# Layer-norm scalars and router steps moved from GpSimd to ScalarE and VectorE in a Mamba and mixture-of-experts kernel

## The chip, the cores and the metric

One core of one Trainium2 chip. The time is the device time of one execution, in microseconds, median of several runs. Of the kernel before three runs were timed: 4454.32 us median, 4450.94 to 4455.48.

## What is computed

```python
x = x + 0.5 * ffn(layernorm(x))        # x: 16 sequences of 512 tokens, 128 wide
x = x + mamba(layernorm(x))            # 4 layers, state 16, inner width 256, then @ Wout + bout
x = x + 0.5 * ffn(layernorm(x))

def layernorm(x):                      # no weights
    return (x - mean(x)) / sqrt(var(x) + 1e-5)
def ffn(x):                            # 8 experts, 2 of them per token, hidden 344
    logits = x @ Ws + bs
    w, idx = top_k(logits, 2);  w = softmax(w)
    combine = sum(one_hot(idx, 8) * w[..., None], axis=1)
    ...                                # silu(x Wg) * (x Wu), then Wd, weighted by combine
def mamba_layer(x):
    ...                                # rmsnorm, Win, causal conv, silu, Wx, softplus
    h = exp(delta * A) * h + (delta * u) * B;  y = h . C      # along the 512 tokens
    ...                                # y * silu(z) @ Wblk, added to x
```

## The kernel before

All inputs are laid out on the host, all weights stay in SBUF. One program runs three kinds of work through the same five in-order queues.

**The scans.** Each of the 16 sequences has 4 Mamba layers: 64 phases of 128 "ticks", one after the other. A phase has 8 units of 4 tiles (128 x 512 each). For a unit, POOL (GpSimd) multiplies delta*u by B (L962, 128 x 2048, signal `dbu_ready`), ACT (ScalarE) makes exp(delta*A) of each tile into one of three PSUM banks (L609), DVE (VectorE) scans each tile (L778), POOL (L953) or, for 12 of the 32 tiles, DVE (L783) multiplies by C, and PE (TensorE) sums into y (L449).

**The feed-forward units.** 32 of them (two per sequence), each 8 experts of 32 ticks: PE broadcasts the expert's gate (L458, "gb"), DVE scales the input by it (L851, "xs"), PE makes g and u tiles (L466, L475, L480) in two PSUM banks a and b in turn, ACT takes silu (L637, between two table loads), DVE multiplies (L858), PE multiplies by Wd (L487).

**The norms and the router.** 48 layer norms: DVE bn_stats and bn_aggr (L866, L872), then four dependent POOL instructions of 128 x 4 (`norm_pool`, L970 to L976: add eps, power -0.5, times mean, times -1), then ACT applies scale and shift (L648). Each of the 32 units begins with such a norm, a transpose on PE (L431), a copy on ACT (L659), the logits on PE (L500, into PSUM bank `s_ps`), and the router: DVE adds the bias (L885), takes the top values (L892, `mx_sb`) and their indices (L897, `mi_sb`); POOL subtracts the two top values (L983, "gap"), converts the indices to float (L985), makes the softmax denominator (L988) after ACT's exponential (L662); DVE inverts it (L908) and compares the indices with 0..7 in two instructions (L903); POOL combines them in nine more steps (L991 to L1010), splitting each weight into three bf16 parts for PE (L507).

**What sets the order.** Nothing is scheduled at run time. Every engine's program is one loop over ticks; the tables `CORE`, `PREP`, `NEAR`, `POST`, `FFN_AT`, `START` and `END` say at which tick each step is issued, so they only set the order on each queue; semaphores do the rest. `NEAR` and `POST_NEAR` serve the first and last two sequences, whose layers follow each other more closely. All PE work that is neither an expert's nor the y sum shares the one bank `s_ps`: `fill("s", signal, n)` makes the next user wait until the last one's reader has signalled. After the logits the next user is the mean of squares of the following phase (L526, "ms").

Of the kernel before, what the change touches and what calls it, by code (L numbers as in the profile page):

```python
# [14 lines left out]
TB = T // 128  # L15
# [16 lines left out]
CORE = {"exp": -10, "scan": -1, "dbu": -12, "dve_prod": 1, "pool_prod": 12, "sum": 30, "y0": 88, "y1": 8}  # L32
PREP = {"dc1": 83, "dc0": 60, "sq": -20, "ms": -6, "rms": -10, "xn": -4, "xp0": 17, "conv0": 16, "xp1": 25, "conv1": 23,
        "silu_xc": 27, "z0": 105, "zc0": 97, "z1": 114, "zc1": 106, "silu_z": 123, "wx": 46, "dbc": 38, "rows": 32, "dt0": 48,
        "sp0": 52, "delta0": 57, "du0": 60, "dt1": 77, "sp1": 71, "delta1": 76, "du1": 79, "dd0": 63, "dd1": 135, "bc": 98}
NEAR = {"dc1": 97, "dc0": 84, "sq": 14, "ms": 28, "rms": 24, "xn": 33, "xp0": 48, "conv0": 48, "xp1": 56, "conv1": 55,
        "silu_xc": 59, "z0": 115, "zc0": 98, "z1": 116, "zc1": 105, "silu_z": 123, "wx": 68, "dbc": 62, "rows": 44, "dt0": 82,
        "sp0": 74, "delta0": 79, "du0": 79, "dt1": 86, "sp1": 86, "delta1": 90, "du1": 91, "dd0": 100, "dd1": 146, "bc": 85}
POST = {"x1": 35, "wblk": 92, "h": 91, "attn": 110, "x2": 105}
POST_NEAR = {"x1": -69, "wblk": 18, "h": 13, "attn": 29, "x2": 40}  # L40
# [166 lines left out]
def build(nc, x, norm_w, Win, conv_w, conv_b, conv_rows, Wx, Wdt, bdt, A_log, Dp, Wblk, Wout, bout,  # L207
          Ws, bs, Wg, Wu, Wd, out, bc_rows, x1):
    with ExitStack() as ctx:
# [33 lines left out]
        neg_half = sb("neg_half", [128, TB])  # L243
# [22 lines left out]
        bn_sb = sb("bn_sb", [128, TB, 6])  # L266
        mv_sb = sb("mv_sb", [128, TB, 2])
        rs_sb = sb("rs_sb", [128, 4, TB])
# [5 lines left out]
        mi_sb = sb("mi_sb", [128, TB, E], U32)  # L274
        mf_sb = sb("mf_sb", [128, TB, 2])
# [143 lines left out]
        def _(pe):  # L419
# [71 lines left out]
            def start_pe(t):  # L491
# [4 lines left out]
                if (f := UNIT_OF.get(t - START["lg"])) is not None:  # L496
                    ps = fill("s", lg_ready, f + 1)
# [100 lines left out]
        def _(act):  # L598
# [499 lines left out]
```

## Time and profile before

| | |
|---|---|
| median of 3 runs | 4454.32 us |
| the profiled execution's own time | 4447.92 us |
| its span | 4446.2 us |
| busy share of the span | DVE 89%, POOL 89%, PE 87%, ACT 75% |
| instructions | PE 12736, DVE 5441, ACT 4991, POOL 1740 |

The profile is of one execution. Busy times are those of the engines' own instructions; "idle before" is time in which an engine waited, put down to what released it last. From 900 to 3720 us the kernel repeats itself every four phases, some 256 us, in which two feed-forward units and three norms lie.

### The profile page before, as it was taken

Reading aid. Unit: us, or ns where it says so; the run is one execution under the profiler, and the core shown is the slowest. Engines: PE = TensorE matmul, PEld = TensorE weight load, DVE = VectorE, ACT = ScalarE, POOL = GpSimd, SP = SyncE. Lnnn points to the kernel's source line nnn. Section 1 sums busy time; section 2 is a strip of 40 time slices with the busy share of each in tenths; the row PEclk is TensorE's granted clock in tenths of the full one; section 3 lists DMA queues with packets and bytes.
Section 4 is the critical chain, followed back from the end, with each engine's and each line's share of the span. In section 5 each row is a group of like instructions: output and inputs, shape, how many; then the busy total and the mean of one; then the engine's idle time right before and its main releaser. Section 6 shows DMA issues by size and latency. Waiting matters only on the chain.

```text
span 4446.2 us, 50132 instructions
## 1 busy us (share of the span) xinstructions
PE 3866.4 (87%) x12736; PEld 1277.6 (29%) x12736; DVE 3971.1 (89%) x5441; ACT 3327.9 (75%) x4991; POOL 3950.6 (89%) x1740
## 2 busy tenths in 40 slices
PE   6786877999999999999999999999999999678868
PEld 2221222232323323332232333223232323122223
DVE  2669999999999999999999999999999999999963
ACT  4567777877878787877878787887878777677744
POOL 0559999999999999999999999999999999999950
PEclk9898888999999999999999999999999999799979
DMA  2234554445444543444454445444544454434410
GB/s 77 60 81 99 115 117 97 96 108 117 94 98 112 112 96 92 116 108 102 96 116 100 97 101 122 96 102 103 117 94 95 113 116 94 112 95 111 94 34 5
DMA packets 151917, 434.67 MB, mean 98 GB/s; under 512 B 16402, under 2 KB 50451, under 8 KB 151124
## 3 DMA queue, kind: packets, MB, share of 16 engines
q1 hardware_dynamic: 151636, 431.46, 41.9%
q8 instruction: 111, 1.82, 0.2%
q14 instruction: 170, 1.39, 0.1%
HBM read 150.38 MB, written 12.58 MB: 37 GB/s over the span
## 4 chain that ended last, share of the span: by engine, by line
PE 39%; DVE 24%; issue 15%; POOL 12%; ACT 9%; DMA 1%; SPq 0%; DVEq 0%; ACTq 0%; POOLq 0%
DVE work L778 10%; POOL work L962 6%; PE d_ps L487 6%; POOL work L953 5%; PE s_ps L534 4%; DVE dA_ps L778 4%; PE y_ps L449 4%; PE b_ps L480 4%; PE a_ps L466 4%; DVE work L783 3%; PE a_ps L480 3%; PE s_ps L567 2%; DVE sg_sb L858 2%; PE b_ps L466 2%; ACT L637 2%
## 5 line engine op out<-in xcount | busy, mean ns | idle before, releaser
L962 POOL TENSOR_TENSOR work<-dd_sb,bc_sb 128x2048 f32<-128x2048 f32 x512 | 2327.9, 4547 | 49.3 <-DMA dd_sb<-dd_src 49.3
L609 ACT ACTIVATE dA_ps<-dd_sb,a_sb 128x512 f32<-128x512 f32 x2048 | 1367.3, 684 | 554.6 <-DVE work L783 290.1
L953 POOL TENSOR_TENSOR work<-work,bc_sb 128x1024 f32<-128x1024 f32 x640 | 1511.3, 2368 | 46.9 <-DVE work L778 46.5
L778 DVE TENSOR_TENSOR_SCAN work<-dA_ps,work 128x512 f32<-128x512 f32 x1280 | 1495.0, 1205 | 51.8 <-POOL work L962 41.4
L778 DVE TENSOR_TENSOR_SCAN dA_ps<-dA_ps,work 128x512 f32<-128x512 f32 x768 | 935.0, 1217 | 6.3 <-ACT dA_ps L609 4.8
L487 PE MATMUL d_ps<-sg_sb,wd_sb 128*128 128x512 f32 x1408 | 648.4, 593 | 4.8 <-DVE sg_sb L858 4.8
L449 PE MATMUL y_ps<-work,sel_sum 128*32 128x512 f32 x4096 | 578.2, 636 | 83.2 <-POOL work L953 56.3
L783 DVE TENSOR_TENSOR work<-dA_ps,bc_sb 128x512 f32<-128x512 f32 x768 | 523.2, 681 | 8.1
L466 PE MATMUL a_ps<-xT_sb,wg_sb 128*128 128x512 f32 x768 | 427.9, 640 | 113.0 <-ACT sg_sb L637 103.1
L466 PE MATMUL b_ps<-xT_sb,wg_sb 128*128 128x512 f32 x640 | 358.3, 642 | 59.0 <-DVE xs_sb L851 55.2
L637 ACT ACT_TABLE_LOAD x256 | 328.4, 1283 | 70.7 <-PE d_ps L487 66.5
L487 PEld LDWEIGHTS d_ps<-sg_sb,wd_sb 128*128 128x128 f32 x1408 | 263.4, 190 | 337.7 <-issue 293.7
L858 DVE TENSOR_TENSOR sg_sb<-sg_sb,b_ps 128x512 f32<-128x512 f32 x384 | 257.8, 671 | 112.0 <-PE b_ps L475 63.4
L638 ACT ACT_TABLE_LOAD x270 | 346.4, 1283 | 4.9
L480 PE MATMUL b_ps<-xs_sb,wu_sb 128*128 128x512 f32 x512 | 287.7, 644 | 4.1 <-ACT sg_sb L637 2.3
L637 ACT ACTIVATE sg_sb<-a_ps 128x512 f32<-128x512 f32 x384 | 228.5, 595 | 78.7 <-PE a_ps L466 70.0
L480 PE MATMUL a_ps<-xs_sb,wu_sb 128*128 128x512 f32 x512 | 283.5, 636 | 1.0 <-ACT sg_sb L637 0.9
L858 DVE TENSOR_TENSOR sg_sb<-sg_sb,a_ps 128x512 f32<-128x512 f32 x320 | 215.7, 674 | 45.0 <-PE a_ps L480 23.1
L534 PE MATMUL s_ps<-xn_pad,wconv_sb 128*128 128x512 f32 x512 | 239.6, 611 | 0.8 <-ACT gates_sb L667 0.8
L637 ACT ACTIVATE sg_sb<-b_ps 128x512 f32<-128x512 f32 x320 | 190.5, 595 | 66.3 <-PE b_ps L466 64.8
L466 PEld LDWEIGHTS a_ps<-xT_sb,wg_sb 128*128 128x128 f32 x768 | 134.2, 194 | 359.6 <-ACT sg_sb L637 197.0
L550 PE MATMUL s_ps<-dbc_sb,wdt_sb 97*128 97x512 f32 x256 | 148.1, 661 | 89.3 <-ACT dd_src L738 61.6
(122 smaller groups left out, 4059.1 us busy)
## 6 DMA issues: line engine op xcount, KB each, us to landing
dd_sb<-dd_src SPq DMA_DIRECT2D x512, 512.0 KB, 8.5
bc_sb<-bc_rows SPq DMA_DIRECT2D x256, 512.0 KB, 5.3
xr_sb<-in_L_attn_x SPq DMA_DIRECT2D x16, 256.0 KB, 3.1
x<-xr_sb SPq DMA_DIRECT2D x16, 256.0 KB, 6.9
bc_rows<-dbc_sb SPq DMA_DIRECT2D x128, 32.0 KB, 1.7
xr_sb<-x SPq DMA_DIRECT2D x16, 256.0 KB, 2.9
out<-xr_sb SPq DMA_DIRECT2D x16, 256.0 KB, 6.9
wg_sb<-in_L_ffn_Wg SPq DMA_DIRECT2D x1, 1408.0 KB, 7.1
```

What stands on the lines that cost most here:

```text
L449: last = pe.matmul(y_ps[SEL * c:SEL * (c + 1), :], sel_sum[:, :], work[:, g % RING, c % 2, :], start=False, stop=(j == NJ - 1))
L466: pe.matmul(ps[:, :], wg_sb[:, tile_number(e, ft), :], xT_sb[:, f % 2, :], start=True, stop=True).then_inc(g_full, 1)
L480: pe.matmul(ps[:, :], wu_sb[:, tile_number(e, ft), :], xs_sb[:, e % 2, :], start=True, stop=True).then_inc(u_full, 1)
L487: last = pe.matmul(d_ps[:, :], wd_sb[:, tile_number(e, ft), :], sg_sb[:, ft, :], start=(tile_number(e, ft) == 0), stop=(e == E - 1 and ft ...
L534: last = pe.matmul(ps[:, :], wconv_sb[:, PHASE[w][1], tap, :], xn_pad[:, tap:tap + T], start=(tap == 0), stop=(tap == KC - 1))
L609: act.activation(dA_ps[:, g % NDA, :], dd_sb[:, b, c, 0, :], ACT.Exp, scale=a_sb[:, l, b, j, c:c + 1]).then_inc(dA_ready, 1)
L637: act.activation(sg_sb[:, ft, :], ps_of[job_bank(x, g_job(x, ft))][:, :], ACT.Silu).then_inc(sg_ready, 1)
L778: dve.tensor_tensor_scan(dA if on_dve(i) else tile, dA, tile, 0.0, ALU.mult, ALU.add).then_inc(scanned, 1)
L783: dve.tensor_tensor(work[:, (g // 2) % RING, g % 2, :], dA_ps[:, g % NDA, :], bc_sb[:, (i // NG) % NJ, 0, :], ALU.mult).then_inc(dve_prod, 1)
L858: dve.tensor_tensor(sg_sb[:, ft, :], sg_sb[:, ft, :], ps_of[job_bank(x, u_job(x, ft))][:, :], ALU.mult).then_inc(hh_ready, 1)
L953: pool.tensor_tensor(work[:, g % RING], work[:, g % RING], bc_sb[:, j, 0, :].unsqueeze(1).broadcast_to([128, 2, T]), ALU.mult).then_inc(po ...
L962: pool.tensor_tensor(work[:, g % RING:g % RING + 2].rearrange("p h c t -> p (h c) t"), dd_sb[:, b, :, 1, :], bc_sb[:, j, 1, :].unsqueeze(1 ...
```

## The change

The norm's scalars go from POOL to ACT as ln, negated mean, exp(-0.5 ln) and four products of one column each; the statistics get two buffers. The router's top-two difference goes into ACT's exponential (four one-column instructions with scale -1 and a bias), the denominator to ACT. The indices are written into the upper half of the logits' PSUM bank, as integers, and DVE compares them in one instruction of 64 elements; with that the bank is free only after the compare (`eq_ready`) and not after the bias (`lg_ready`). POOL keeps seven steps of the router. All order tables have new numbers; of `START`, which is for the unit's beginning, and `PREP`, for a layer's preparation, a part is shown.

```diff
-START = {"load": -96, "bn": -59, "nb": -53, "xtok": -46, "xt": -29, ... "lg_sb": -34, "mx": -33,
-         "mi": -31, "gap": -32, "we": -30, "eq": -24, "den": -32, "inv": -27, "comb": -24, "ct": -10, "gates": -24}
+START = {"load": -96, "bn": -60, "ln": -57, "rs": -55, "nb": -55, "xtok": -53, "xt": -36, ... "lg_sb": -35, "mx": -35,
+         "mi": -35, "we": -37, "eq": -33, "den": -35, "inv": -32, "comb": -40, "ct": -25, "gates": -23}
-PREP = {"dc1": 83, ... "wx": 46, "dbc": 38, "rows": 32, "dt0": 48, ... "sp1": 71, "delta1": 76, "du1": 79,
+PREP = {"dc1": 77, ... "wx": 37, "dbc": 41, "rows": 71, "dt0": 45, ... "sp1": 67, "delta1": 75, "du1": 77,
...
+        mi_ps = s_ps[:, TB * E:2 * TB * E].bitcast(U32).rearrange("p (k e) -> p k e", e=E)
...
-                    ps = fill("s", lg_ready, f + 1)
+                    ps = fill("s", eq_ready, f + 1)
...
+            def log_act(what, f):
+                m = NORM_OF[what, f]
+                act.wait_ge(mv_done, m + 1)
+                if m > 1:
+                    act.wait_ge(xtok_ready, m - 1)
+                act.activation(rs_sb[:, m % 2, 0, :], mv_sb[:, m % 2, :, 1], ACT.Ln, bias=eps_sb[:, 0:1])
+                act.activation(rs_sb[:, m % 2, 1, :], mv_sb[:, m % 2, :, 0], ACT.Copy, scale=-1.0).then_inc(var_log, 1)
+            def rstd_act(what, f):
+                m = NORM_OF[what, f]
+                act.wait_ge(var_log, m + 1)
+                act.activation(rs_sb[:, m % 2, 0, :], rs_sb[:, m % 2, 0, :], ACT.Exp, scale=-0.5).then_inc(rstd_done, 1)
+            def shift_act(what, f):
+                m = NORM_OF[what, f]
+                act.wait_ge(rstd_done, m + 1)
+                for k in range(TB):
+                    last = act.activation(rs_sb[:, m % 2, 2, k:k + 1], rs_sb[:, m % 2, 1, k:k + 1], ACT.Copy,
+                                          scale=rs_sb[:, m % 2, 0, k:k + 1])
+                last.then_inc(nb_ready, 1)
...
-                    act.wait_ge(gap_ready, f + 1)
-                    act.activation(wt_sb[:, 1, :], wt_sb[:, 0, :], ACT.Exp).then_inc(we_ready, 1)
+                    act.wait_ge(mx_ready, f + 1)
+                    for k in range(TB):
+                        last = act.activation(wt_sb[:, 1, k:k + 1], mx_sb[:, k, 0:1], ACT.Exp, scale=-1.0, bias=mx_sb[:, k, 1:2])
+                    last.then_inc(we_ready, 1)
+                if (f := UNIT_OF.get(t - START["den"])) is not None:
+                    act.wait_ge(we_ready, f + 1)
+                    act.activation(wt_sb[:, 2, :], wt_sb[:, 1, :], ACT.Copy, scale=2.0, bias=2.0).then_inc(den_ready, 1)
...
-                        last = dve.max_index(mi_sb[:, k, :], mx_sb[:, k, :], lg_sb[:, k, :])
+                        last = dve.max_index(mi_ps[:, k, :], mx_sb[:, k, :], lg_sb[:, k, :])
...
-                    for i in range(2):
-                        at_i = mf_sb[:, :, i].unsqueeze(2).broadcast_to([128, TB, E])
-                        last = dve.tensor_tensor(eq_sb[:, i], iota_e[:, :].unsqueeze(1).broadcast_to([128, TB, E]), at_i,
-                                                 ALU.is_equal)
+                    mi_i = mi_ps[:, :, 0:2].rearrange("p k i -> p i k").unsqueeze(3).broadcast_to([128, 2, TB, E])
+                    dve.tensor_tensor(eq_sb[:, :, :, :], mi_i,
+                                      iota_e[:, :].unsqueeze(1).unsqueeze(1).broadcast_to([128, 2, TB, E]),
+                                      ALU.is_equal).then_inc(eq_ready, 1)
...
-            def norm_pool(what, f):
...
-                    for i in range(2):
-                        w_i = wt_sb[:, 3 + i, :].unsqueeze(2).broadcast_to([128, TB, E])
-                        pool.tensor_tensor(eq_sb[:, i], eq_sb[:, i], w_i, ALU.mult).then_inc(rt_step, 1)
+                    w_i = wt_sb[:, 3:5, :].unsqueeze(3).broadcast_to([128, 2, TB, E])
+                    pool.tensor_tensor(eq_sb[:, :, :, :], eq_sb[:, :, :, :], w_i, ALU.mult).then_inc(rt_step, 1)
```

Where the instructions stand now, at three places. First DVE at the beginning of a feed-forward unit, from the logits on, before:

```order
L778 SCALAR_TENSOR_TENSOR work<-dA_ps,work 128x512 x2
L885 TENSOR_TENSOR lg_sb<-s_ps,bs_sb 128x32
L892 MAX mx_sb<-lg_sb 128x8 x4
L778 SCALAR_TENSOR_TENSOR dA_ps<-dA_ps,work 128x512
L897 MAX_INDEX mi_sb<-mx_sb,lg_sb 128x8 x4
L783 TENSOR_TENSOR work<-dA_ps,bc_sb 128x512
L851 TENSOR_TENSOR xs_sb<-xT_sb,b_ps 128x512
L778 SCALAR_TENSOR_TENSOR dA_ps<-dA_ps,work 128x512
L908 RECIPROCAL wt_sb<-wt_sb 128x4
L816 TENSOR_TENSOR xn_pad<-h_sb,s_ps 128x512
L783 TENSOR_TENSOR work<-dA_ps,bc_sb 128x512
L903 TENSOR_TENSOR eq_sb<-iota_e,mf_sb 128x32 x2
```

and after the change:

```order
L815 SCALAR_TENSOR_TENSOR work<-dA_ps,work 128x512 x2
L922 TENSOR_TENSOR lg_sb<-s_ps,bs_sb 128x32
L929 MAX mx_sb<-lg_sb 128x8 x4
L934 MAX_INDEX s_ps<-mx_sb,lg_sb 128x8 x4
L941 TENSOR_TENSOR eq_sb<-s_ps,iota_e 128x64
L948 RECIPROCAL wt_sb<-wt_sb 128x4
L815 SCALAR_TENSOR_TENSOR dA_ps<-dA_ps,work 128x512
L820 TENSOR_TENSOR work<-dA_ps,bc_sb 128x512
L888 TENSOR_TENSOR xs_sb<-xT_sb,b_ps 128x512
```

The whole router now stands in one block ahead of the scan that stood after the maxima (the rows of L778 and L815 are the scans). Second PE at the same place, with what each row waits for, before:

```order
L500 MATMUL s_ps<-ws_sb,xT_sb 128x8 x3
L526 MATMUL s_ps<-xpad,mean_w 128x512 [waits sq_ready,lg_ready]
L466 MATMUL a_ps<-xT_sb,wg_sb 128x512 [waits xT_ready,hh_ready]
L458 MATMUL b_ps<-gates_sb,sel_gate 128x512 [waits gates_ready,hh_ready]
L449 MATMUL y_ps<-work,sel_sum 32x512 [waits dve_prod,pool_prod]
```

and after the change:

```order
L497 MATMUL s_ps<-ws_sb,xT_sb 128x8 x3
L523 MATMUL s_ps<-xpad,mean_w 128x512 [waits sq_ready,eq_ready]
L463 MATMUL a_ps<-xT_sb,wg_sb 128x512 [waits xT_ready,hh_ready]
L455 MATMUL b_ps<-gates_sb,sel_gate 128x512 [waits gates_ready,hh_ready]
L446 MATMUL y_ps<-work,sel_sum 32x512 [waits dve_prod,pool_prod]
```

The order is the same; the mean of squares waits for the compare instead of the bias, and the last expert's gate stands two places behind it. Third ACT, from the end of the seventh expert's silu to the logits' input, after the change (before, the five rows of L654 to L666 and L689 to L693 were not there, and one exponential more stood ahead of `xtok` and of `xT_sb`):

```order
L635 ACT_TABLE_LOAD
L606 ACTIVATE dA_ps<-dd_sb,a_sb 128x512
L654 ACTIVATE rs_sb<-mv_sb,eps_sb 128x4
L655 ACTIVATE rs_sb<-mv_sb 128x4
L660 ACTIVATE rs_sb<-rs_sb 128x4
L666 ACTIVATE rs_sb<-rs_sb 128x1 x4
L760 ACTIVATE zs_sb<-s_ps 128x512
L606 ACTIVATE dA_ps<-dd_sb,a_sb 128x512
L645 ACTIVATE xtok<-xr_sb,rs_sb 128x128 x4
L606 ACTIVATE dA_ps<-dd_sb,a_sb 128x512
L760 ACTIVATE zs_sb<-s_ps 128x512
L606 ACTIVATE dA_ps<-dd_sb,a_sb 128x512
```

Seven small instructions stand between two exponentials that the scans wait for.

## Rows read from the trace of the kernel before

**Rows 1.** Stretch; busy PE, PEld, DVE, ACT, POOL; granted clock, DMA share, GB/s
```profile
900.00:3720.00 2820.00, 2588.46 (x8765) 860.42 (x8763) 2711.91 (x3734) 2251.68 (x3404) 2719.40 (x1190) 0.99 0.46 104
```
**Rows 2.** DVE's waits, 900 to 3720 us: total, times, longest
```profile
DVE lg_sb L885 <- PE s_ps L500: 26.2, 22, 3.0
DVE xr_sb L808 <- PE s_ps L577: 19.6, 11, 1.8
DVE sg_sb L858 <- PE b_ps L480: 12.9, 37, 0.4
...
DVE work L778 <- POOL work L962: 9.3, 11, 1.0
...
DVE xs_sb L851 <- PE b_ps L458: 3.3, 3, 1.4
DVE work L778 <- ACT dA_ps L609: 2.2, 13, 0.2
```
**Rows 3.** POOL's waits, 900 to 3720 us
```profile
POOL wt_sb L983 <- DVE mx_sb L892: 17.4, 11, 2.6
POOL mf_sb L985 <- DVE mi_sb L897: 15.9, 11, 1.4
...
POOL wt_sb L988 <- ACT wt_sb L662: 7.3, 22, 0.4
```
**Rows 4.** Groups of instructions, whole span: count, busy us, mean ns, idle before
```profile
L953 POOL TENSOR_TENSOR work<-work,bc_sb 128x1024 f32<-128x1024 f32 x640 | 1511.3, 2368 | 46.9 <-DVE work L778 46.5
L778 DVE TENSOR_TENSOR_SCAN work<-dA_ps,work 128x512 f32<-128x512 f32 x1280 | 1495.0, 1205 | 51.8 <-POOL work L962 41.4 <-ACT dA_ps L609 9.2
...
L972 POOL TENSOR_TENSOR rs_sb<-rs_sb,neg_half 128x4 f32<-128x4 f32 x48 | 49.8, 1038 | 4.0
...
L903 DVE TENSOR_TENSOR eq_sb<-iota_e,mf_sb 128x32 f32<-128x32 f32 x64 | 15.0, 275 | 0.0
...
L976 POOL TENSOR_SCALAR rs_sb<-rs_sb 128x4 f32<-128x4 f32 x48 | 11.3, 235 | 4.2
...
L970 POOL TENSOR_SCALAR rs_sb<-mv_sb 128x4 f32<-128x4 f32 x48 | 10.9, 227 | 196.4 <-DVE mv_sb L872 191.1 <-ACT xtok L648 1.9
...
L974 POOL TENSOR_TENSOR rs_sb<-mv_sb,rs_sb 128x4 f32<-128x4 f32 x48 | 9.7, 203 | 3.8
...
L662 ACT ACTIVATE wt_sb<-wt_sb 128x4 f32<-128x4 f32 x32 | 6.4, 200 | 23.6 <-POOL wt_sb L983 23.6
```
**Rows 5.** PE's waits, 900 to 3720 us
```profile
PE s_ps L567 <- ACT dd_src L738: 24.9, 44, 0.9
...
PE s_ps L550 <- ACT dbc_sb L745: 21.2, 44, 0.5
```
**Rows 6.** One router in order of time, DVE: start, us, work, idle before
```profile
2119.75 0.19 DVE L885 TENSOR_TENSOR lg_sb<-s_ps,bs_sb 128x32 f32<-128x32 f32 x1 [0.63 <-PE s_ps L500]
2119.98 0.37 DVE L892 MAX8 mx_sb<-lg_sb 128x8 f32<-128x8 f32 x4
...
2121.39 0.07 DVE L897 MATCH_VALUE_LOAD mi_sb<-mx_sb,lg_sb 128x8 f32 x1
...
2121.85 0.16 DVE L897 FIND_INDEX8 mi_sb<-mx_sb,lg_sb 128x8 uint32<-128x8 f32 x1
...
2122.51 0.68 DVE L851 TENSOR_TENSOR xs_sb<-xT_sb,b_ps 128x512 f32<-128x512 f32 x1
```
**Rows 7.** The same router on PE
```profile
2118.68 1.03 PE L500 MATMUL s_ps<-ws_sb,xT_sb 128*128 128x8 f32 x8 [0.78 <-ACT xT_sb L659]
2120.00 1.13 PE L526 MATMUL s_ps<-xpad,mean_w 128*128 128x512 f32 x2 [0.28 <-DVE lg_sb L885]
...
2121.91 0.39 PE L458 MATMUL b_ps<-gates_sb,sel_gate 24*128 24x512 bf16 x1
```
**Rows 8.** The router 254 us later, PE
```profile
2374.56 2.04 PE L526 MATMUL s_ps<-xpad,mean_w 128*128 128x512 f32 x2 [0.28 <-DVE lg_sb L885]
```
**Rows 9.** Busy time by stretch at that router, columns as in rows 1
```profile
2376.00:2380.00 4.00, 4.00 (x13) 0.88 (x12) 2.57 (x12) 3.31 (x6) 3.56 (x5) 0.75 1.00 220
```

More of the change, by code:

```diff
@@ L31 @@
 W, PERIOD = 128, 32
[L32 to L40, printed above, removed]
@@ L41 @@
-FFN_AT = {"gb": 7, "xs": 3, "g0": 5, "g1": 9, "g2": 9, "burst": 5, "u0": 13, "u1": 18, "u2": 26, "hh0": 14, "hh1": 15,
-          "hh2": 21, "down": 32}
-START = {"load": -96, "bn": -59, "nb": -53, "xtok": -46, "xt": -29, "xT": -39, "lg": -29, "lg_sb": -34, "mx": -33,
-         "mi": -31, "gap": -32, "we": -30, "eq": -24, "den": -32, "inv": -27, "comb": -24, "ct": -10, "gates": -24}
-END = {"yt": 27, "xo": 33, "bn": 47, "nb": 60, "xtok": 67, "ht": 89, "h": 76, "store": 90, "acc": 4}
+CORE = {"exp": -11, "scan": -1, "dbu": -23, "dve_prod": 1, "pool_prod": -2, "sum": 22, "y0": 84, "y1": 7}
@@ new lines @@
+PREP = {"dc1": 77, "dc0": 59, "sq": -17, "ms": -14, "rms": -9, "xn": -2, "xp0": 13, "conv0": 16, "xp1": 18, "conv1": 22,
+        "silu_xc": 27, "z0": 99, "zc0": 96, "z1": 109, "zc1": 103, "silu_z": 123, "wx": 37, "dbc": 41, "rows": 71, "dt0": 45,
+        "sp0": 49, "delta0": 57, "du0": 60, "dt1": 65, "sp1": 67, "delta1": 75, "du1": 77, "dd0": 124, "dd1": 190, "bc": 137}
+NEAR = {"dc1": 93, "dc0": 79, "sq": 11, "ms": 19, "rms": 23, "xn": 31, "xp0": 41, "conv0": 48, "xp1": 44, "conv1": 54,
+        "silu_xc": 59, "z0": 99, "zc0": 97, "z1": 110, "zc1": 105, "silu_z": 123, "wx": 65, "dbc": 63, "rows": 68, "dt0": 72,
+        "sp0": 74, "delta0": 81, "du0": 81, "dt1": 80, "sp1": 86, "delta1": 91, "du1": 98, "dd0": 76, "dd1": 142, "bc": 75}
@@ L265, in build @@
         acc_sb = xtok[:, :, :].rearrange("p k d -> p (k d)")
[L266 to L268 removed]
+        bn_sb = sb("bn_sb", [128, 2, TB, 6])
+        mv_sb = sb("mv_sb", [128, 2, TB, 2])
+        rs_sb = sb("rs_sb", [128, 2, 3, TB])
         xT_sb = sb("xT_sb", [128, 2, T])
@@ L648, in norm_act @@
                     last = act.activation(xtok[:, k, :], xr_sb[:, x_slot(FFN[f][1], n), k, :], ACT.Identity,
-                                          scale=rs_sb[:, 0, k:k + 1], bias=rs_sb[:, 2, k:k + 1])
+                                          scale=rs_sb[:, m % 2, 0, k:k + 1], bias=rs_sb[:, m % 2, 2, k:k + 1])
                 last.then_inc(xtok_ready, 1)
-            def start_act(t):
+            def log_act(what, f):
[16 more added lines that the diff above has]
+                last.then_inc(nb_ready, 1)
+            def start_act(t):
+                if (f := UNIT_OF.get(t - START["ln"])) is not None:
+                    log_act("start", f)
+                if (f := UNIT_OF.get(t - START["rs"])) is not None:
+                    rstd_act("start", f)
+                if (f := UNIT_OF.get(t - START["nb"])) is not None:
+                    shift_act("start", f)
                 if (f := UNIT_OF.get(t - START["xtok"])) is not None:
@@ L669, in end_act @@
             def end_act(t):
+                if (f := UNIT_OF.get(t - E * PERIOD - END["ln"])) is not None and FFN[f][1] == 1:
+                    log_act("ln2", f)
+                if (f := UNIT_OF.get(t - E * PERIOD - END["rs"])) is not None and FFN[f][1] == 1:
+                    rstd_act("ln2", f)
+                if (f := UNIT_OF.get(t - E * PERIOD - END["nb"])) is not None and FFN[f][1] == 1:
+                    shift_act("ln2", f)
                 if (f := UNIT_OF.get(t - E * PERIOD - END["acc"])) is not None:
@@ L865, in norm_dve @@
                 for k in range(TB):
-                    last = dve.bn_stats(bn_sb[:, k, :], xr_sb[:, x_slot(FFN[f][1], n), k, :])
+                    last = dve.bn_stats(bn_sb[:, m % 2, k, :], xr_sb[:, x_slot(FFN[f][1], n), k, :])
                 last.then_inc(bn_done, 1)
                 dve.wait_ge(bn_done, m + 1)
-                if m > 0:
-                    dve.wait_ge(shift_done, m)
+                if m > 1:
+                    dve.wait_ge(nb_ready, m - 1)
                 for k in range(TB):
-                    last = dve.bn_aggr(mv_sb[:, k, :], bn_sb[:, k, :])
+                    last = dve.bn_aggr(mv_sb[:, m % 2, k, :], bn_sb[:, m % 2, k, :])
                 last.then_inc(mv_done, 1)
```

78 lines of the change are left out of this document (29 added, 49 removed).

## The prediction

> **What bounds the kernel now.** I read the busy time by stretch first. Between 900 and 3720 us, 11 repeats of some 256 us, POOL works 2719.4 of 2820 us, DVE 2711.9, PE 2588.5 and ACT 2251.7 [rows 1]: POOL 96.4%, DVE 96.2%. Busy shares don't tell which of two such engines paces the other, so I read next who waits for whom in that stretch. DVE is idle for 2820 - 2711.9 = 108 us, and only 9.3 us of that is for POOL's products; the largest items are for PE (26.2 us for the logits, 19.6 us for the output projection, 12.9 us for expert tiles in one bank) [rows 2]. POOL is idle for 101 us, 17.4 + 15.9 + 7.3 = 40.6 us of it inside the router, for DVE and ACT [rows 3]. So POOL is as full as DVE, but it is hardly ever the one that is waited for. DVE sets the pace, and PE, which is in order, tells it when it may go on. That is the reading on which all that follows rests: time taken from POOL is worth what DVE waits for POOL.
>
> **The change part by part**, over the whole program (32 routers, 48 norms).
>
> *POOL.* Removed are the norm's 49.8 + 11.3 + 10.9 + 9.7 = 81.7 us busy [rows 4] and five small router steps; at the 0.2 us of the norm's smallest [rows 4] these are 32 x 5 x 0.2 = 32 us. That makes 114 us, besides the 40.6 us of waiting [rows 3]. On the path lies only DVE's wait for POOL: 41.4 us in the whole span [rows 4], 9.3 us of it in the steady stretch [rows 2]. The steady part should vanish; the rest, at the ends, is where POOL itself waits for a first transfer or for the layer before, and I count a quarter of it. Bounds: 9.3 and 41.4; I take -17.
>
> *DVE, the compare.* Two instructions cost 15.0 us in 32 routers, 0.47 us each time [rows 4]. One of 64 elements, with an operand in PSUM, is not shown; it lies between one of the old, 0.27 us, and both, 0.47 us. I take 0.30, nearer the one since the elements are few: -5.
>
> *The bank is held longer.* This is the term against the change. The mean of squares on PE started at 2120.00, 0.06 us after the bias ended at 2119.94 [rows 6, 7]. Now it waits for the compare. The maxima end 0.41 us after the bias, the indices take 0.62 us (2121.39 to 2122.01) [rows 6], the compare 0.30, and each of the steps waits for the one before, some 0.05 us: the bank is free 1.42 us later. PE's gate for the last expert, which ended at 2122.30 [rows 7], ends at 2123.72. DVE, after its block of the router (now with the reciprocal), the scan and the product, reaches xs at about 2123.15 and starts it at 2123.82, as against 2122.51 [rows 6]. Of these 1.31 us, 0.5 are compare and reciprocal done earlier than before; 0.8 us are lost, in 32 routers 26 us. Bounds: nothing, if PE is ahead by then; 0.8 + 1.4 us, if PE's clock falls as well (below), 70 us. I take +26.
>
> *PE ahead of the logits.* The new tables issue delta's second half and its copy one scan earlier and the block matmul behind the gate; PE's waits there (24.9 us for the copy at L567, 21.2 us at L550, 44 times each, about 0.5 us a phase [rows 5]) should partly go. They stand ahead of the logits in PE's order, and DVE waits for the logits 26.2 / 22 = 1.2 us each time [rows 2]. One such wait, 24.9 / 44 = 0.57 us, in each of 32 routers is -18; bounds 0 and (24.9 + 21.2) x 64 / 44 = 67. The projection of the last layer stands earlier on PE, but so does its sum on DVE, and both lie in one stretch that PE fills to the logits: what DVE saves there (19.6 us) it waits at the logits. I count it as nothing. The same moves should take a third of DVE's waits for expert tiles in that bank (12.9 us in the steady stretch [rows 2], x 64 / 44 = 19 in all): -6, bounds 0 and 19.
>
> *ACT.* New are 48 x 7 + 32 x 4 = 464 instructions. At the 0.20 us of the exponential of 128 x 4 [rows 4] this is 93 us. ACT has 568 us free in the steady stretch alone [rows 1], and DVE waited for its exponentials 2.2 us there [rows 2]. But seven of them, 1.4 us, stand between two exponentials, with three PSUM banks as the only lead. Bounds: 0, and 48 x 1.4 = 67 if DVE felt each; the lead covered table loads and three silus ahead of this place, so I take +5.
>
> The Trainium skill, "ScalarE: Activation LUTs", rules for kernel authors, speaks against this part: additions and products belong on VectorE. By that rule the sum would hold the seven on DVE, at the 0.09 us that each of the four maxima took (0.37 us together [rows 6]): 48 x 7 x 0.09 = 30 us on the engine with 4% free, in place of my 5 on ACT. The busy times [rows 1] decide for ACT here, whatever an element costs.
>
> *SP and the ends.* On SP's queue the second delta transfer now stands behind the fourth B/C transfer, which waits for POOL's last product of the phase before; it is needed four units later, and these units hide it, so I count nothing; uncovered it would cost one POOL product of 2.4 us [rows 4] in each of 64 phases, 152 us. Where norm and router are uncovered, in a few units at the ends, the four POOL steps take 1.70 us by their means [rows 4], ACT's seven 1.4, and the router saves a change of engine or two: -2.
>
> The sum is -17 - 5 + 26 - 18 - 6 + 5 - 2 = -17. The profiled execution took 4447.9 us, so 4431; the median of the runs is 6.4 us above it, which gives **4437 us**. From no change a measurement of this kernel tells 0.2%, 9 us.
>
> **The rivals.**
>
> *PE's clock falls at the routers (slower).* At the router of 2120 PE had waited 0.78 and 0.28 us around the logits and went on at full speed: 1.13 us for the mean of squares [rows 7]. At that of 2374 the mean of squares took 2.04 us [rows 8] and the granted clock was 0.75 over 4 us [rows 9], that is, in half of it 1.2 in place of 2.4 GHz. DVE then stands up to 1.4 us at xs; that happened 3 times in 22 steady routers [rows 2]. With PE idle 1.4 us longer at this place it may happen at most of them. If at all 32: 32 x 1.4 = 45 us on top of the sum, +28, a median of 4482. It decides from the point where 17 / 1.4 = 12 more routers fall. For it: the idle stretch more than doubles. Against it: ACT's mean of squares and the experts behind leave slack, and PE waits for others all along. The Trainium skill, "TensorE: Matmul & The Clock Gate", Part 1, says that the array returns to the lower clock after an idle stretch and regains the full one only by sustained work. By that rule this rival would be the likely case; the trace agrees where the clock fell, and shows DVE held at 3 of 22 only.
>
> *POOL paces after all.* Then the freed 114 us and the 40.6 us of waits come back until DVE is full, at most DVE's 108 us. With half of that, 54 us, and the other terms near zero in sum, 4400. For it: POOL's 96.4%. Against it: DVE's 9.3 us.
>
> *Nothing moves.* The terms cancel to within 9 us, or the new order brings DVE new small waits in place of the old: 4454. For it: seven terms of a few microseconds, of both signs.
>
> **How the numbers follow.** Forecast 0.33 (4437, itself between 4418 and 4445), POOL as the pace 0.15, nothing 0.20, the clock or another new wait 0.32. Faster by over 0.2%: 0.33 + 0.15 = 0.48; within: 0.20; slower: 0.32. The forecast's and the other cases' unknown bounds (the bank 0 to 70, PE's lead 0 to 67, ACT 0 to 67) don't fall out together; a range of 4388 to 4488 takes in the clock's 4482 and POOL's 4400 and leaves out the ends of both, about 0.1 each.
>
> **What would show it.** Right: POOL's busy share falls by 3% and DVE's wait for POOL is gone, while POOL's idle time grows by about what was removed; DVE stays the fullest engine; the mean of squares waits about 1.7 us for the compare instead of 0.28; DVE waits at xs of the eighth expert; the wait for the logits shrinks below 1.2 us; ACT's small instructions take 0.2 us and DVE waits for exponentials less than 10 us. Wrong: a lower granted clock and matmuls of 1 us behind every router (the slower rival), or four phases that take 250 us or less with POOL never idle (POOL paced). If DVE waits for exponentials next to the norm, ACT's term was too small.

## The result and the profile after

The changed kernel took **4509.0 us** (median of 4; 4505.7 to 4514.0) where the one before took 4454.6: a ratio of 1.0130, 95% interval 1.0115 to 1.0145. It is 54 us slower by these medians, 58 by the ratio. The forecast was 17 us faster with a range up to 4488, so it was wrong in sign, and the range did not hold the result.

Busy time over the whole span, from the page:

```profile
PE 3895.1 (86%) x12736; PEld 1286.3 (29%) x12736; DVE 3992.8 (89%) x5408; ACT 3413.7 (76%) x5455; POOL 3846.4 (85%) x1388
```

POOL lost 104 us of work (3950.6 before) and PE and DVE got more of it, though DVE has 33 instructions fewer and PE the same ones. Where the loss lies is seen in ten whole repeats, from the first scan of phase 12 to that of phase 52 (columns as in [rows 1]), before and after:

```profile
975.82:3535.13 2559.31, 2348.52 (x7961) 780.73 (x7960) 2462.20 (x3391) 2044.68 (x3092) 2468.88 (x1080) 0.99 0.46 104
```

```profile
980.72:3595.30 2614.58, 2379.41 (x7961) 793.91 (x7960) 2482.01 (x3372) 2098.64 (x3381) 2404.45 (x861) 0.98 0.44 102
```

55.3 of the 57.7 us by which the profiled span grew are there; ramp and end came out nearly level. PE's account: the same 7960 matmuls took 30.9 us longer, at a lower granted clock, and PE was idle 24.4 us longer. DVE's account: 19.8 us more work, 35.5 more waiting. DVE's waits in 900 to 3720 us show at whom:

```profile
DVE xs_sb L888 <- PE b_ps L455: 37.1, 32, 2.2
DVE s_ps L865 <- ACT s_ps L751: 25.1, 43, 0.7
DVE lg_sb L922 <- PE s_ps L497: 18.9, 22, 0.9
DVE sg_sb L895 <- PE a_ps L472: 11.8, 24, 1.7
DVE sg_sb L895 <- PE b_ps L477: 10.5, 31, 0.3
DVE dA_ps L815 <- ACT dA_ps L606: 5.0, 11, 0.5
...
DVE xr_sb L845 <- PE s_ps L574: 3.2, 11, 0.5
```

Against [rows 2]: the wait for POOL is gone, those for the logits (26.2 us) and the output projection (19.6) have shrunk, exponentials cost 6 us. Two waits are new or nearly so: at xs, for the expert's gate (3.3 before), and 0.6 us in each phase at the first tap of the convolution (L865; 4.1 in all before). PE's waits and POOL's in the same stretch, against [rows 3, 5]:

```profile
PE s_ps L547 <- ACT dbc_sb L782: 71.8, 43, 1.9
PE s_ps L523 <- DVE eq_sb L941: 36.0, 22, 1.6
```

```profile
POOL work L992 <- DVE work L815: 212.2, 159, 2.8
```

The wait of PE's block matmul for ACT's copy of delta (L567 before, 24.9 us) is gone; that for dbc, the copy of the scan parameters, has grown by 50. POOL's relief became waiting for DVE's scans (26.0 us before).

**The convolution.** The first tap before (rows of DVE and ACT in order of time), then after:

```profile
1305.00 0.69 DVE L783 TENSOR_TENSOR work<-dA_ps,bc_sb 128x512 f32<-128x512 f32 x1
...
1305.51 0.75 ACT L714 ACTIVATE s_ps<-s_ps,cb_sb,cw_sb 128x512 f32<-128x512 f32 x1
1305.61 0.68 DVE L851 TENSOR_TENSOR xs_sb<-xT_sb,a_ps 128x512 f32<-128x512 f32 x1
...
1306.29 0.76 DVE L828 SCALAR_TENSOR_TENSOR s_ps<-xpad,cw_sb,s_ps 128x512 f32<-128x512 f32 x1
```

```profile
1317.85 0.69 DVE L820 TENSOR_TENSOR work<-dA_ps,bc_sb 128x512 f32<-128x512 f32 x1
...
1318.36 0.75 ACT L751 ACTIVATE s_ps<-s_ps,cb_sb,cw_sb 128x512 f32<-128x512 f32 x1
...
1319.14 0.76 DVE L865 SCALAR_TENSOR_TENSOR s_ps<-xpad,cw_sb,s_ps 128x512 f32<-128x512 f32 x1 [0.60 <-ACT s_ps L751]
...
1319.80 0.68 DVE L888 TENSOR_TENSOR xs_sb<-xT_sb,a_ps 128x512 f32<-128x512 f32 x1
```

The expert's input scaling, which covered ACT's instruction, now stands behind the tap: DVE waits 0.60 us, and xs, for which PE waits, comes later too. The tables do this (xs 3 to 4, conv1 23 to 22), in 55 of 64 phases.

**A router** after, where the clock fell (order of time), and the granted clock behind it:

```profile
2149.27 0.19 DVE L922 TENSOR_TENSOR lg_sb<-s_ps,bs_sb 128x32 f32<-128x32 f32 x1 [0.86 <-PE s_ps L497]
...
2150.59 0.22 DVE L941 TENSOR_TENSOR eq_sb<-s_ps,iota_e 128x64 f32<-128x64 uint32 x1
...
2150.87 2.07 PE L523 MATMUL s_ps<-xpad,mean_w 128*128 128x512 f32 x2 [1.64 <-DVE eq_sb L941]
...
2152.74 1.91 PE L463 MATMUL a_ps<-xT_sb,wg_sb 128*128 128x512 f32 x2
...
2155.22 0.69 DVE L888 TENSOR_TENSOR xs_sb<-xT_sb,b_ps 128x512 f32<-128x512 f32 x1 [2.17 <-PE b_ps L455]
```

```profile
2150.80:2154.70 3.90, 3.83 (x5) 1.27 (x5) 2.01 (x4) 2.46 (x5) 3.46 (x9) 0.50 0.00 0
```

The mean of squares starts 1.41 us after the bias ends; at a granted clock of 0.50, that is 1.2 GHz, it takes 2.07 us in place of 1.13 [rows 7], and DVE stands 2.17 us at xs. In the steady stretch that happened in full at 6 of 22 routers (2 before).

### The profile page after: what moved, and what is told of

Read it like the earlier page. It is cut to its first block, busy times and chain, and to the rows that moved or that the text cites. A ratio compares the mean times of both kernels' runs of the same rounds, so it can differ in the third digit from the quotient of the medians.

```text
span 4503.9 us, 50303 instructions
## 1 busy us (share of the span) xinstructions
PE 3895.1 (86%) x12736; PEld 1286.3 (29%) x12736; DVE 3992.8 (89%) x5408; ACT 3413.7 (76%) x5455; POOL 3846.4 (85%) x1388
## 4 chain that ended last, share of the span: by engine, by line
PE 43%; DVE 23%; issue 13%; ACT 12%; POOL 7%; DMA 1%; SPq 1%; DVEq 0%; ACTq 0%; POOLq 0%
DVE work L815 10%; PE d_ps L484 8%; DVE dA_ps L815 5%; PE s_ps L531 5%; PE y_ps L446 4%; PE a_ps L463 4%; PE b_ps L477 3%; PE b_ps L463 3%; POOL work L1001 3%; POOL work L992 3%; PE a_ps L477 3%; ACT dA_ps L606 3%; DVE work L820 2%; ACT L634 2%; PE s_ps L541 2%
## 5 line engine op out<-in xcount | busy, mean ns | idle before, releaser
L815 DVE TENSOR_TENSOR_SCAN work<-dA_ps,work 128x512 f32<-128x512 f32 x1280 | 1490.7, 1205 | 35.9 <-POOL work L1001 29.8
L815 DVE TENSOR_TENSOR_SCAN dA_ps<-dA_ps,work 128x512 f32<-128x512 f32 x768 | 936.1, 1219 | 16.1 <-ACT dA_ps L606 13.0
L484 PE MATMUL d_ps<-sg_sb,wd_sb 128*128 128x512 f32 x1408 | 673.2, 610 | 8.6 <-DVE sg_sb L895 8.6
```

The costliest lines, as they stand in the source:

```text
L484: last = pe.matmul(d_ps[:, :], wd_sb[:, tile_number(e, ft), :], sg_sb[:, ft, :], start=(tile_number(e, ft) == 0), stop=(e == E - 1 and ft ...
L815: dve.tensor_tensor_scan(dA if on_dve(i) else tile, dA, tile, 0.0, ALU.mult, ALU.add).then_inc(scanned, 1)
```

## The experiments

Each kernel ran beside the one before on one chip (medians in us). "Old" and "new" order are the tables before and after.

| kernel | what it is | median | before beside it | ratio, 95% interval |
|---|---|---|---|---|
| steps_only | new steps, old order | 4518.7 | 4448.9 | 1.0155, 1.0141 to 1.0168 |
| order_only | old steps, new order | 4478.7 | 4448.9 | 1.0072, 1.0058 to 1.0086 |
| conv_behind_xs | changed, taps back | 4466.9 | 4448.9 | 1.0040, 1.0026 to 1.0054 |
| order_conv | order_only, taps back | 4456.6 | 4450.5 | 1.0015, 1.0006 to 1.0024 |
| conv_only | before, taps ahead of xs | 4486.6 | 4449.4 | 1.0075, 1.0061 to 1.0089 |
| hold_only | before, bank held | 4494.7 | 4452.8 | 1.0099, 1.0084 to 1.0114 |
| steps_old_index | steps_only, old index path | 4468.6 | 4452.8 | 1.0038, 1.0025 to 1.0052 |
| bank_early | changed, indices in SBUF | 4522.5 | 4448.9 | 1.0156, 1.0142 to 1.0170 |
| steps_ms | steps_only, ms behind a gate tile | 4531.1 | 4450.5 | 1.0176, 1.0162 to 1.0190 |
| conv_ms | conv_behind_xs, the same | 4464.5 | 4450.5 | 1.0036, 1.0022 to 1.0050 |
| conv_old_index | conv_behind_xs, old index path | 4475.5 | 4449.4 | 1.0057, 1.0044 to 1.0071 |
| norm_only | before, norm on ACT | 4473.6 | 4452.8 | 1.0047, 1.0034 to 1.0061 |
| norm_behind_z | norm_only, norm behind z's copy | 4460.2 | 4448.5 | 1.0026, 1.0017 to 1.0035 |
| steps_mended | steps_old_index, the same | 4464.8 | 4448.5 | 1.0034, 1.0024 to 1.0044 |
| conv_ms_dbc | conv_ms, dbc earlier | 4482.9 | 4450.5 | 1.0072, 1.0058 to 1.0086 |
| order_pairs | order_conv, pairs back | 4503.1 | 4452.8 | 1.0110, 1.0094 to 1.0126 |
| early_out2 | before, output projection earlier | 4451.7 | 4449.4 | 1.0003, 0.9994 to 1.0012 |
| early_out | and y, h with it | 4452.9 | 4449.4 | 1.0006, 0.9997 to 1.0015 |

### Steps or order

```diff
 steps_only: tables of before; START and END gain "ln", "rs", "nb", "den" of ACT,
             "mi": -31 -> -33, "eq": -24 -> -33 (behind the maxima)
 order_only: code of before; tables of after, its own POOL steps kept in place
```

> The changed norm and router in the old order: every table keeps its old numbers, so PE and SP issue exactly what they issued before; only the norm's seven small instructions stand on ACT, the router's indices and compare stand together behind the maxima, and the logits' bank is held until the compare. Theory ORDER (the new tables cost the time: the first convolution tap on DVE now stands directly behind the product and waits 0.6 us for ACT in each of 64 phases, 38 us, and 150 more products follow their scan directly, 0.1 us each): 4435 to 4465, about as before. Theory BANK (the bank that is held until the compare costs it: DVE waits for the expert's gate 27 us at 17 of 22 steady routers, some 39 us in 32): 4480 to 4500.

> The old norm and router in the new order: all tables but the router's and the norm's own steps have the new numbers; POOL makes the norm and its five router steps as before, and the logits' bank is free when the bias is added. Theory ORDER: 4490 to 4515, nearly the changed kernel's time, with DVE waiting 0.6 us at the first tap of each convolution. Theory BANK: 4450 to 4475.

Both are slower alone, by 70 and 30 us, and together only 54. In steps_only PE's order is untouched, and the router is where it is lost: DVE waits 43.5 us at xs (21 times), and the mean of squares runs slow at 19 of 21 routers. One of them:

```profile
2159.16 2.07 PE L523 MATMUL s_ps<-xpad,mean_w 128*128 128x512 f32 x2 [1.64 <-DVE eq_sb L941]
...
2161.27 0.66 ACT L734 ACTIVATE s_ps<-s_ps,eps_sb 128x512 f32<-128x512 f32 x1 [3.73 <-PE s_ps L523]
...
2163.12 0.69 DVE L888 TENSOR_TENSOR xs_sb<-xT_sb,b_ps 128x512 f32<-128x512 f32 x1 [2.15 <-PE b_ps L455]
```

ACT's queue stands 3.73 us behind the same matmul. Each theory names the wait that its half shows: BANK that at xs, ORDER that at the tap (30.3 us in order_only, 4.1 before). But steps_only came out above BANK's range and order_only between the two, so neither covers both halves, and the two prices don't add up.

### The taps

```diff
 conv_behind_xs, order_conv:  PREP  - "conv1": 22   + "conv1": 23
 conv_only (from before):     FFN_AT  - "xs": 3  + "xs": 4;  PREP  - "conv1": 23  + "conv1": 22
```

> The changed kernel with one number changed: the DVE taps of the convolution are issued one tick later, so that the input scaling of the expert stands ahead of the first tap again, as it did before; nothing moves on the other engines. Theory ORDER: the wait of 0.6 us in 64 phases goes, 38 us of the changed kernel's 4509: 4465 to 4480. Theory BANK, or a wait that comes back at the next place on DVE: 4495 to 4509.

> The old steps in the new order (4478.7 us), with the convolution's taps on DVE one tick later, behind the input scaling of the expert, as in the changed kernel with one number changed (4466.9 us, 42 below the changed kernel). Theory CONV (the first tap's wait is the only thing in the new order that costs): 4433 to 4445. Rival (the convolution's wait hid another, as PE's wait for the copy of delta's inputs): 4455 to 4475.

> The kernel before with two numbers changed: on DVE the first tap of the convolution and the second half of delta stand ahead of the expert's input scaling, as the change has it; steps, engines and the other queues are the old ones. Theory ADD (the tap's wait of 0.6 us in some 55 phases is a price of its own): 25 to 42 above the kernel before, 4475 to 4495. Theory TOGETHER (it costs only with the new steps, or DVE makes it good at the logits): within 12 us of before.

One number takes the ratio of the changed kernel from 1.0130 to 1.0040, 40 us, into ORDER's range; alone, the two numbers make the kernel before 37 us slower, as ADD said. Ten repeats of conv_only, of conv_behind_xs and of order_only (columns as in [rows 1]):

```profile
985.69:3579.84 2594.15, 2377.61 (x7961) 788.98 (x7960) 2459.55 (x3392) 2045.45 (x3092) 2468.15 (x1080) 0.98 0.45 103
```

```profile
974.99:3559.57 2584.58, 2351.09 (x7959) 786.24 (x7960) 2484.60 (x3372) 2093.93 (x3381) 2402.75 (x861) 0.99 0.45 103
```

```profile
978.63:3557.39 2578.76, 2353.01 (x7961) 787.02 (x7960) 2471.94 (x3391) 2044.27 (x3092) 2470.21 (x1081) 0.99 0.45 103
```

In conv_only DVE's wait at the tap grew by 24 us and that for the logits by 14; PE's matmuls took 29 us longer (2377.6 against 2348.5) and PE was idle 6 longer: the expert's gate projections wait for the bank that xs reads (46.9 us in 900 to 3720, 29.6 before). In conv_behind_xs, where PE waits for the compare as long as in the changed kernel, the matmuls are down from 2379.4 to 2351.1 us while PE is idle as long (233.5 against 235.2): the slow matmuls of the change went almost all with the taps. But in the new order they need the new steps too: in order_only, with the taps ahead and the old steps, the matmuls take 2353.0 us.

So the taps are worth 24 us with the old steps, and part of the 40 is owed to the company of the new ones. order_conv came out 6 us above before, in the rival's range and short of the 4433 to 4445 that CONV expected. The wait for dbc stayed (57.0 us), but that it makes the 6 us is not shown.

### The held bank

```diff
 hold_only (from before):  - fill("s", lg_ready, f + 1)   + fill("s", mi_ready, f + 1);  START "mi": -31 -> -33
 steps_old_index:  indices in SBUF, POOL makes them float, two compares at START "eq": -24; fill on lg_ready
 conv_old_index:   the same in conv_behind_xs
 bank_early (from after):  - mi_ps = s_ps[...]   + mi_sb = sb("mi_sb", [128, TB, E], U32);  fill on lg_ready
 steps_ms, conv_ms:  PREP "ms": -6 -> -4, -14 -> -12 (behind g0 of the last expert)
```

> The kernel before, all steps and engines as they were, with the logits' bank held by a semaphore until the indices are found, and the indices issued right behind the maxima, ahead of one scan: the mean of squares on PE starts some 1.1 us later in 32 units, and nothing else is added. Theory HOLD: 4480 to 4515 (that hold is four fifths of the 1.36 us that cost some 70). Theory STEPS: 4445 to 4458.

> The new steps in the old order (4518.7 us) but for the path of the indices, which is the old one: they lie in SBUF, POOL makes them float, DVE compares them in two instructions, and the logits' bank is free when the bias has been added. The norm, the exponential and the denominator stay on ACT, POOL keeps 8 steps. Theory HOLD (the bank held until the compare is what costs the 70 us): 4440 to 4455, level with the kernel before. Theory STEPS (the small instructions on ACT, or POOL and DVE waiting for them, cost it): 4490 to 4520.

With the bank held 1.1 us longer, and the indices one scan earlier on DVE, the kernel before loses 42 us, as HOLD said, and DVE's wait at xs (3.3 us in [rows 2]) becomes:

```profile
DVE xs_sb L851 <- PE b_ps L458: 41.8, 22, 2.6
```

With the old path of the indices, steps_only comes down from 70 us above the kernel before to 16, between the ranges of HOLD and STEPS. In the old order the hold is the steps' main cost; 16 us remain.

> The changed kernel with the indices in SBUF in place of the logits' bank: the compare reads them there, and the bank is free when the bias has been added, so that the mean of squares on PE starts some 1.5 us earlier in 32 units; all orders stay. Theory ORDER: 4495 to 4509. Theory BANK: 4470 to 4485, with PE's clock back at its upper level behind the router and DVE's wait for the gate below 0.5 us there.

It came out above both ranges, on something else. The compare, now with both operands in SBUF, waited inside itself for POOL:

```profile
2146.66 2.33 POOL L992 TENSOR_TENSOR work<-work,bc_sb 128x1024 f32<-128x1024 f32 x1
...
2147.44 1.64 DVE L941 TENSOR_TENSOR eq_sb<-mi_sb,iota_e 128x64 f32<-128x64 uint32 x1
```

It lasted until POOL's product was over, 1.64 us; with the indices in PSUM it took 0.21 to 0.23 us at all 32 routers, beside such a product too. DVE's wait at xs did go, as BANK said (3.1 us in 900 to 3720, 37.1 in the changed kernel), but the 32 compares took 40.4 us in place of 7.2. So this run doesn't price the hold. (The Trainium skill, "SBUF — State Buffer", section on the two separate sides, says that a DVE instruction with two SBUF inputs and a GpSimd instruction that reads SBUF exclude each other for the whole instruction; the two rows agree.)

> The new steps in the old order (4518.7 us), with one number changed: on PE the mean of squares of the next phase is issued behind the gate projection of the last expert and no longer ahead of it, so that PE works while DVE makes indices and compare; all other orders stay. Theory HOLD (the bank held 1.4 us longer leaves PE idle, its clock falls, and DVE waits 2.07 us for the expert's gate at every router, 66 us in 32): 4450 to 4465, with the mean of squares at the upper clock and DVE's wait at the expert's input below 0.7 us. Theory STEPS (the new small instructions on ACT and the changed waits of POOL cost the 70 us by themselves): 4500 to 4520, since nothing of theirs moves.

> The changed kernel with both numbers changed, the taps behind the input scaling and the mean of squares behind the gate projection. Theory HOLD: the 20 us that DVE still waits for the expert's gate in the steady stretch with the first change alone go for the most part, 22 to 29 us in the whole: 4438 to 4450, faster than or level with the kernel before. Theory STEPS: 4460 to 4470.

HOLD missed twice. steps_ms came out above both ranges; conv_ms lies in STEPS' range, level with conv_behind_xs (1.0036 against 1.0040), though DVE's wait at xs fell from 20.1 us to 4.4. In steps_ms PE had a gate tile to do, and still:

```profile
2162.81 1.10 PE L463 MATMUL a_ps<-xT_sb,wg_sb 128*128 128x512 f32 x2
...
2164.59 1.97 PE L523 MATMUL s_ps<-xpad,mean_w 128*128 128x512 f32 x2 [0.68 <-DVE eq_sb L941]
...
2166.59 0.66 ACT L734 ACTIVATE s_ps<-s_ps,eps_sb 128x512 f32<-128x512 f32 x1 [3.62 <-PE s_ps L523]
```

DVE's wait at xs fell as expected (to 0.73 us behind this router), but the mean of squares was still slow, at 20 of 21 routers (19 of 21 in steps_only), ACT still waited 3.6 us for it, and what stands behind on ACT, the silus, was late: DVE then waited 41 us for the up tiles. As these rows read, what the hold delays is a chain, mean of squares, ACT's queue, silu, tiles, and filling PE's gap doesn't shorten it; no run tests the chain by itself.

> The changed kernel with the taps moved back (18 us above the one before) and the old path of the indices (SBUF, POOL makes them float, two compares on DVE, the bank free when the bias has been added). Theory HOLD EVERYWHERE: 12 to 40 us less than with the taps alone, 4430 to 4455. Theory HOLD ABSORBED (in the new order the logits and the out projection come earlier, and PE has slack there): within 6 us of it, 4460 to 4472.

In the new order the old path is no better, 8 us worse, above both ranges. That HOLD costs nothing there is not shown by it: the old path brings its own waits. In 900 to 3720 us DVE stands 10.5 us at the reciprocal (4.6 in conv_behind_xs), and PE waits 21.7 us for the gate parts that POOL makes (none over 0.15 us in conv_behind_xs).

### The norm

```diff
 norm_only (from before): norm_pool -> log_act, rstd_act, shift_act; START "ln": -56, "rs": -54, "nb": -54
 norm_behind_z, steps_mended: "ln": -52, "rs": -50, "nb": -50
```

> The kernel before with the norm's arithmetic on ACT alone, seven small instructions in 48 norms in place of POOL's four; the router and every order are the old ones. Theory HOLD: 4438 to 4455, POOL's 82 us of work less and DVE's waits unchanged. Theory STEPS: 4465 or more, with DVE waiting for exponentials behind the norm.

It takes 82 us from POOL and loses 21: STEPS' time, but not for its reason. In ten repeats DVE's wait for POOL went (8 us), and that for the logits grew by 16. Late are not the exponentials but ACT's copy of z, which frees the bank for PE's output projection:

```profile
2249.06 0.86 ACT L668 ACTIVATE rs_sb<-rs_sb 128x1 f32<-128x1 f32 x4
2249.82 0.57 ACT L755 ACTIVATE zs_sb<-s_ps 128x512 f32<-128x512 f32 x1
...
2250.45 0.49 PE L575 MATMUL s_ps<-wout_sb,h_sb 128*128 128x128 f32 x2 [0.70 <-ACT zs_sb L755]
...
2253.88 0.69 DVE L840 TENSOR_TENSOR xr_sb<-xr_sb,s_ps 128x512 f32<-128x512 f32 x1 [2.55 <-PE s_ps L576]
```

DVE waits 2.55 us for the projection; 1.8 was the longest before [rows 2].

> The kernel with the norm alone on ACT (20 us above the one before), the seven small instructions issued behind ACT's copy of z and one exponential later, as late as the scaling that needs them allows; the other queues stay. Theory COPY (the seven hold up the copy that frees the shared bank, so PE's output projection and the logits come late and the clock falls behind the wait): the wait of 0.70 us goes, 4445 to 4458. Theory COUNT (464 more small instructions on ACT cost what they last, wherever they stand): within 6 us of 4473.

> All new steps in the old order, with the old path of the indices and the norm behind the copy of z. POOL has 8 router steps and no norm. Theory COPY: 4437 to 4452, the steps' gain at the ends (5 to 8 us) left over. Theory COUNT: within 6 us of 4468.

The wait of 0.70 us went, the wait for the projection is back at 19.6 us in 11, and the ratio fell from 1.0047 to 1.0026: COPY is some 9 of the 21 us, as far as two intervals that just touch can tell, and norm_behind_z lies between the two ranges. The logits' wait stayed (40.0 us, 26.2 before), and in steps_mended nothing was won within its interval, which is COUNT's range. The rest of the norm's price stays open: in norm_behind_z the same matmuls still take 15 us longer than before in ten repeats (2363.6), while PE is idle no longer (209.0, 210.8 before).

### Other waits of the new order

```diff
 conv_ms_dbc:  PREP "dbc": 41 -> 40
 order_pairs (from order_conv):  CORE "y0": 84 -> 88; POST "h": 87 -> 91; PREP "xn": -2 -> -4
 early_out2 (from before):  POST "attn": 110 -> 98, "x2": 105 -> 97
 early_out:  POST "wblk": 93, "h": 87, "attn": 94, "x2": 93; CORE "y0": 84
```

> The kernel of the two changed numbers with a third: ACT's copy of the scan parameters (dbc) is issued one exponential earlier, as it was before. PE's wait for that copy should fall from 56 us to about 21 in the steady stretch. If DVE feels it: 5 to 15 us less than without this; if it is hidden by what PE has in hand: within 4 us of it.

PE's wait for dbc fell to 14 us, and the kernel got 18 us slower, which neither case had: DVE waited 20 us for one kind of up tile, 8 before this number was changed. Why is open.

> The old steps in the new order with the taps moved back (4456.6 us), and three more numbers of DVE's order set back: the y gate, the residual sum and the norm's product stand between a scan and the product that reads it, where they stood before. Products directly behind their scan fall from 330 to 239. Theory OVERLAP (such a product starts some 0.1 us later, since it reads what the scan has just written): 91 x 0.096 = 9 us less, 4445 to 4450. Rival (the order of these pairs is worth nothing): 4453 to 4460.

The pairs gave what OVERLAP said, and more: in ten repeats 60 products left the place behind their scan, and the products' time beyond the end of the instruction before them fell by 9.3 us (0.73 us each behind the scan, 0.60 elsewhere). But the residual sum, one of the three, feeds the output projection, which the new order has early: DVE waited 50.6 us for it (under 3 in order_conv). The price of a pair is measured; the kernel lost 44 us against order_conv and missed both ranges.

> The kernel before with two numbers changed: the output projection of the last layer stands two places earlier on PE, ahead of the first up projection of the expert, and its sum two scans earlier on DVE. DVE waited 17.8 us for it in ten repeats. Theory WAIT (that wait goes and comes back nowhere): 18 to 28 us less than before, 4422 to 4435. Theory PACE (PE sets the pace, so DVE waits elsewhere as long): within 9 us of before.

> The same with the y gate, the residual sum and the block matmul moved as the change has them too, which puts 36 more products directly behind their scan (0.1 us each). Theory WAIT: 4425 to 4440. Theory PACE: within 9 us of before.

early_out2 was too small a step: DVE waits 20.3 us, as before. early_out removed the wait and got nothing; its DVE waits:

```profile
DVE lg_sb L885 <- PE s_ps L500: 29.0, 22, 1.4
DVE sg_sb L858 <- PE b_ps L480: 15.9, 44, 0.4
...
DVE xr_sb L808 <- PE s_ps L577: 4.6, 11, 0.5
```

Ten repeats of it (2559.31 us before):

```profile
980.24:3540.90 2560.66, 2337.32 (x7961) 784.58 (x7960) 2469.20 (x3392) 2037.02 (x3092) 2468.97 (x1080) 0.99 0.46 104
```

There DVE waits 13.6 us less at the projection, 2.2 more at the logits and 8.2 more at the expert's tiles. In all it waits 5.6 us less, and its own instructions take 7.0 us longer (2462.20 before), in part since 20 more products stand directly behind their scan. Both times are PACE's; its reason, that DVE waits for PE somewhere else, holds for 8 of the 13.6 us. No kernel of the study beats the one before.

## Why the prediction was wrong

**The reading of the bound** was half right. POOL indeed didn't pace: 104 us off it gave nothing. But "time taken from POOL is worth what DVE waits for POOL", -17, fails too: the 9.3 us went, and in norm_only the wait for the logits grew by twice as much. DVE meets PE again a few units later, at the logits, the gate, the expert's tiles, and spends much of what it has saved waiting there: of the 13.6 us that early_out took off the projection, 8 came back as waits.

**The step that failed** is "PE ahead of the logits": it read the new tables for PE's waits alone, -18 and -6, where order_only measured +30. What they moved on DVE, the taps ahead of xs, was not costed at all, and is the largest term that undoing finds in the changed kernel: 37 us alone, 40 by undoing it. The trace of before had the price: ACT's instruction ended at 1306.26, 0.57 us behind the product, and xs filled just that. Of the two waits of PE that it counted, 24.9 us went at the block matmul, and 50.6 came at dbc, one exponential later. What DVE was to gain came in part, and was outweighed: in 900 to 3720 us its wait for the logits fell by 7.3 us, that for the expert's tiles by 6.2.

**The bank** was the best step and the worst price. The mean of squares was to start 1.42 us later; PE's wait ahead of it grew by 1.36 (0.28 to 1.64). The cost of 0.8 us a router, 26 us in all, fits only the upper clock: where the mean of squares ran at full speed in the changed kernel (13 of 22 routers), DVE stood 0.7 us at xs on average; where it ran at the lower clock (6), 2.2 us, as the upper bound (70) had it. All terms but those of the order add up to +7 in the forecast; steps_only lost 70 and hold_only 42. In the new order the price could not be separated.

**ACT**, +5, was sized by the wrong reader. Its small instructions took 0.2 to 0.28 us, and DVE waited 6 us for exponentials, as said; but in the old order the norm costs some 20 us, in part through ACT's copy of z, whose only hurried reader is the next user of the bank that it empties.

The groups of instructions after (columns as in [rows 4]):

```profile
L666 ACT ACTIVATE rs_sb<-rs_sb 128x1 f32<-128x1 f32 x192 | 40.9, 284 | 1.6
...
L693 ACT ACTIVATE wt_sb<-wt_sb 128x4 f32<-128x4 f32 x32 | 6.6, 205 | 1.0
...
L941 DVE TENSOR_TENSOR eq_sb<-s_ps,iota_e 128x64 f32<-128x64 uint32 x32 | 7.2, 224 | 1.1
```

**The compare**, -5, is -7.8 (7.2 in place of 15.0), and mostly not for the reason given: 9 of the old 64 compares, both operands in SBUF, took 0.36 to 1.65 us, each until a running POOL product had ended; the median was 0.18. **The projection's** wait, counted as nothing, was removed (19.6 to 3.2), and early_out, which removes it from the kernel before, gained nothing. The overlap that 150 products lost was in no term: in ten repeats the products' time beyond the end of the instruction before them grew by 13.2 us.

**The rivals.** That the clock falls at the routers, or another new wait comes, given 0.32 and 4482, was the right direction and half the amount. 30.9 of the 55.3 us are slower matmuls, but in this order the routers alone don't make them: 28.3 went in conv_behind_xs, which moves only the taps and holds the bank as long. The range ended 21 us short since no rival priced the tap.

The 58 us of the ratio so split, along one path, as: taps 40, the rest of the new order 6 (order_conv), the rest of the steps 12 (conv_behind_xs less order_conv). Along another path the parts differ, as the 24 us of the taps with the old steps show. In ten repeats conv_behind_xs is 15.1 us longer than order_conv, and 8.8 of these are DVE's own instructions. Which part of the 12 is the norm's and which the bank's is open: a compare in PSUM that frees the logits' bank early was not tried.

## What to carry to other kernels

When a change renumbers an order by hand, list for every engine the pairs of neighbours that it swaps, and ask of each what covered the wait of the second; the price of a cover is read at the instruction that stood there, not at the one that waits. A buffer held longer is priced along the chain that it delays, through the in-order queue of every reader, before one looks at the engine that idles. And a wait removed on one engine counts in full only if that engine doesn't meet the bound engine again before the saving is spent.

## What the runs showed of the hardware

Two things were unexpected. A DVE compare with both operands in SBUF waited for a running POOL instruction, up to 1.65 us in the steady stretch of bank_early and as long in the kernel before; the same compare with one operand in PSUM never did (0.21 to 0.23 us). And whether a matmul ran at the lower clock didn't follow from the wait just ahead of it: behind 1.64 us of waiting the mean of squares took over 1.5 us at 7 of 22 routers of the changed kernel and at 19 of 21 of steps_only; behind a gate tile at full speed and 0.68 us, at 17 of 18 of steps_ms and 7 of 22 of conv_ms; behind 0.28 us, at 2 of 22 before and 7 of 22 of order_conv. What decides it stays open.
